# Attention stage: both exponentials ahead of the keeps, the output weights inside the turning product, sums one batch earlier, and 512 columns of x quantised by VectorE

## What is computed

```python
x = x + tanh(g_xattn[0]) * mlstm(layernorm(x), ctx, ctx, ifgate_w, ifgate_b, outnorm_w)
x = x + tanh(g_ffn[0])   * ffn_int8(layernorm(x), W1, b1, W2, b2)
x = x + tanh(g_xattn[1]) * align_by_time_warping(ctx, layernorm(x))
x = x + tanh(g_ffn[1])   * gated_experts(layernorm(x), ...)

def mlstm(q, k, v, ...):                      # 8 heads of 16 features
    log_d = lf[t] - lf[s] + i_pre[s]          # masked to s <= t
    m = max(log_d); d_mat = exp(log_d - m)
    s_mat = (q @ k.T) / 4 * d_mat
    denom = maximum(abs(sum(s_mat)), exp(-m)) + 5e-5
    h = (s_mat @ v) / denom
    rrms = rsqrt(mean(h * h) + 1e-6)          # per head
    return h * rrms * (1 + outnorm_w)

def qlinear(x, W, b):                         # twice in ffn_int8, gelu between
    scale = max((x.max() - x.min()) / 255, 1e-8)
    zp = clip(round(-x.min() / scale) - 128, -128, 127)
    xq = clip(round(x / scale) + zp, -128, 127)
    return ((xq - zp) @ wq.T) * (scale * sw) + b
```

## Time and profile before

| what | us |
|---|---|
| median of 3 runs (905.22 to 906.47) | 905.29 |
| the profiled execution, its own time | 905.67 |
| its span in the trace | 903.9 |

### The profile page before, as it was taken

One profiled execution on the slowest core, in us unless ns is written; L12 is line 12 of the kernel. 1 busy time (PEld: TensorE's weight loads), 2 busy tenths in 40 slices (PEclk: granted clock), 3 DMA queues, 4 the chain that ended last, 5 costly groups with the idle time before them and its releaser, 6 DMA issues.

```text
span 903.9 us, 16672 instructions
## 1 busy us (share of the span) xinstructions
PE 617.6 (68%) x5953; PEld 437.7 (48%) x6037; DVE 676.0 (75%) x1896; ACT 430.6 (48%) x892; POOL 196.3 (22%) x160
## 2 busy tenths in 40 slices
PE   4957999923425830000170479999999999999998
PEld 3943444411124630000160376777666777777776
DVE  6658467788979659899799875655666778878775
ACT  2425455457762363333560436556554445445543
POOL 3000168611436002221000036777000000000000
PEclk9999999975555985555585758999999999999999
DMA  7000000000001000000040000000000000001000
GB/s 195 24 1 0 2 1 1 2 1 1 1 14 33 1 1 1 9 12 12 14 140 0 1 1 1 2 2 1 1 2 13 2 13 0 12 0 35 0 13 13
DMA packets 20747, 13.12 MB, mean 15 GB/s; under 512 B 1580, under 2 KB 19240, under 8 KB 20680
## 3 DMA queue, kind: packets, MB, share of 16 engines
q1 hardware_dynamic: 20680, 12.27, 4.9%
HBM read 9.12 MB, written 2.10 MB: 12 GB/s over the span
## 4 chain that ended last, share of the span: by engine, by line
PE 55%; DVE 33%; issue 5%; ACT 5%; SPq 1%; DMA 1%; DVEq 0%; POOL 0%; ACTq 0%; POOLq 0%
PE PS L1494 7%; PE PS L1509 6%; PE PS L1511 6%; PE PS L1510 6%; PE PS L1495 6%; DVE Bm L1078 5%; DVE rowm L1090 5%; PE PS L1493 5%; DVE A L1073 4%; PE PS L1268 2%; PE PS L1334 2%; DVE hmm L1015 2%; DVE hmm L1016 2%; DVE A L728 2%; PE PS L1344 2%
## 5 line engine op out<-in xcount | busy, mean ns | idle before, releaser
L691 ACT ACTIVATE A<-PS,small_t 128x512 f32<-128x512 f32 x256 | 168.4, 688 | 123.9 <-PE PS L1495 122.4
L1509 PE MATMUL PS<-kT_w,A 128*128 128x128 bf16 x1024 | 174.8, 219 | 0.0
L1510 PE MATMUL PS<-kT_w,A 128*128 128x128 bf16 x1024 | 174.8, 219 | 0.0
L1511 PE MATMUL PS<-kT_w,A 128*128 128x128 bf16 x1024 | 174.7, 219 | 0.0
L1184 DVE TENSOR_TENSOR A<-A 128x512 bf16<-128x512 f32 x192 | 123.5, 690 | 12.0 <-ACT A L691 10.8
L1446 PE MATMUL PS<-identf,slab 128*128 128x128 f32 x128 | 21.1, 321 | 125.2 <-ACT xn_w L658 121.8
L1509 PEld LDWEIGHTS PS<-kT_w,A 128*128 128x128 bf16 x1024 | 100.2, 98 | 11.3 <-issue 4.6
L1510 PEld LDWEIGHTS PS<-kT_w,A 128*128 128x128 bf16 x1024 | 100.2, 98 | 6.6
L1494 PE MATMUL PS<-A,xn_w 128*128 128x512 bf16 (+1 forms) x256 | 98.2, 384 | 3.6 <-issue 0.4
L1511 PEld LDWEIGHTS PS<-kT_w,A 128*128 128x128 bf16 x1024 | 100.2, 98 | 0.0
L1495 PE MATMUL PS<-A,xn_w 128*128 128x512 bf16 (+1 forms) x256 | 98.3, 384 | 0.0
(11 more groups left out here) (287 smaller groups left out, 1279.1 us busy)
## 6 DMA issues: line engine op xcount, KB each, us to landing
slab<-in_L_ffn_w_dram SPq DMA_DIRECT2D x16, 256.0 KB, 3.1
xs<-in_x_dram SPq DMA_DIRECT2D x4, 512.0 KB, 6.3
cs<-in_ctx_dram SPq DMA_DIRECT2D x4, 512.0 KB, 6.8
out_dram<-xs SPq DMA_DIRECT2D x8, 256.0 KB, 2.3
A<-Bm SPq DMA_DIRECT2D x9, 64.0 KB, 2.0
xn_w<-in_L_ffn_W_dram SPq DMA_DIRECT2D x2, 256.0 KB, 2.9
A<-Bm SPq DMA_DIRECT2D x4, 36.0 KB, 1.8
A<-Bm SPq DMA_DIRECT2D x4, 24.0 KB, 1.8
```

Of the source, the lines that this page charges most:

```text
L691: act.activation(hf[:, e % 2, c, :], bank(c), ACT.Gelu_apprx_tanh, bias=b1).then_inc(S["h_gelu"], 1)
L1509: pe.matmul(o, hh[:, e % 2, c, t], w2h[:, e, c, :], start=(c == 0 and k == 0), stop=False, skip_group_check=True)
L1510: pe.matmul(o, hh[:, e % 2, c, t], w2l[:, e, c, :], start=False, stop=False, skip_group_check=True)
L1511: ins = pe.matmul(o, hl[:, e % 2, c, t], w2h[:, e, c, :], start=False, stop=(c == NC - 1), skip_group_check=True)
```

## The change

1. **ScalarE's order.** keep(b - 2) moves behind weights_exp(b, 1) and keep_turned(b - 1). squares(m) moves from b % 4 == 2 to 1.
2. **The turning product.** A matrix tmat of 128 x 132 for each half is built by GpSimd before the loop: 68 columns of the identity (four heads of 17) and 64 columns of the identity times onw_b. turn becomes two f32 products with it, keep copies 264 columns at a stretch, and each head's values are there plain and multiplied. normed reads the multiplied ones; the pass over onw_b goes, on GpSimd for six blocks and in late_norm for two. oall holds 16 sequences now, used in turn, for which keep waits at every fourth sequence from 16 on. TensorE waits for turn_made ahead of the loop.
3. **Sums one batch earlier** on VectorE: divisors at b % 4 == 1, mean_squares at 2; ln_stats(1, 0) at b = 24. Behind the loop the order is new as well, and TensorE issues turn(30) ahead of weigh(31).
4. **x's quantisation** is cut at 512, 1024, 2048 and 3072. The first 512 columns VectorE does alone in three passes, which raise xq_first; TensorE's first group waits for that. ab2_b's multiplication moves ahead of the loop.
5. **ScalarE** takes one Gelu of one column ahead of scale_x, roots(7) behind the first of its sixteen normalisations and the last square root behind the twelfth.

```diff
+XCUTS = [(512, 1024), (1024, 2048), (2048, 3072), (3072, 4096)]
...
+        oall = Bm[:, 4352:8576].rearrange("p (n w) -> p n w", n=16)
+        tmat = Bm[:, 10240:10504].rearrange("p (s c) -> p s c", s=2)
...
+            ident4 = identf[:].rearrange("p (j w) -> p j w", j=4)
+            for half in range(2):
+                pool.tensor_copy(tmat[:, half, 0:4 * VW].rearrange("p (j w) -> p j w", j=4), ident4[:, :, 0:VW])
             pool.wait_ge(S["gain_ready"], 1)
+            for half in range(2):
+                ins = pool.tensor_tensor(tmat[:, half, 4 * VW:4 * VW + 4 * DH].rearrange("p (j w) -> p j w", j=4), ident4[:, :, 0:DH],
+                                         onw_b[:, 64 * half:64 * half + 64].rearrange("p (j w) -> p j w", j=4), ALU.mult)
+            ins.then_inc(S["turn_made"], 1)
+            pool.wait_ge(S["turn_made"], 1)
...
             def onto(m):
-                t4 = four(osq[:, m % 2])
-                chain(pool.tensor_tensor(t4, t4, rep(onw_b[:], 4), ALU.mult), m, 4)
-                pool.tensor_tensor(g4(xs, m), g4(xs, m), t4, ALU.add).then_inc(S["x2_ready"], 1)
+                pool.tensor_tensor(g4(xs, m), g4(xs, m), four(osq[:, m % 2]), ALU.add).then_inc(S["x2_ready"], 1)
...
+                if b % 4 == 0 and b >= 16:
+                    act.wait_ge(S["x2_ready"], b // 4 - 3)
+                act.activation(oall[:, b % 16, :], bank(7, 0, 264), ACT.Copy).then_inc(S["o_kept"], 1)
...
                 weights_exp(b, 0)
-                if b >= 2:
-                    keep(b - 2)
                 weights_exp(b, 1)
                 if b >= 1:
                     keep_turned(b - 1)
-                if b % 4 == 2 and b >= 6:
+                if b >= 2:
+                    keep(b - 2)
+                if b % 4 == 1 and b >= 5:
                     squares(b // 4 - 1)
...
+            act.activation(gwarm, cst[:, 0:1], ACT.Gelu)
...
+            dve.tensor_tensor(ab2_b[:], ab2_b[:], tg[:, 2:3].to_broadcast([P, D]), ALU.mult)
             dve.wait_ge(S["expnm_ready"], 1)
...
                 if b % 4 == 0 and g >= 3:
-                    x_range(g - 3, 0)
+                    ins = x_range(g - 3, 0)
+                if b == 24:
+                    link(ins)
+                    ln_stats(1, 0)
+                if b % 4 == 1 and g >= 1:
+                    divisors(g - 1)
                 if b % 4 == 1 and g >= 3:
                     x_range(g - 3, 1)
                 if b % 4 == 2 and g >= 1:
-                    divisors(g - 1)
-                if b % 4 == 3 and g >= 1:
                     mean_squares(g - 1)
...
-                link(dve.tensor_tensor(th, heads(m)[:, :, 0:DH], last(f, DH), ALU.mult))
-                link(dve.tensor_tensor(four(t), four(t), rep(onw_b[:], 4), ALU.mult))
+                link(dve.tensor_tensor(by_head(t), gained(m), spread_out(f), ALU.mult))
...
+            first = xn_w1[:, 0:512]
+            dve.wait_ge(S["ln_half"], 1)
+            link(ts(first, first, qs[:, affine_x:affine_x + 1], MAGIC, ALU.mult, ALU.add))
+            link(ts(first, first, qs[:, affine_x + 2:affine_x + 3], qs[:, affine_x + 3:affine_x + 4], ALU.max, ALU.min))
+            ts(xq[:, 0:512], first, MAGIC, None, ALU.subtract).then_inc(S["xq_first"], 1)
...
+            pe.wait_ge(S["turn_made"], 1)
...
-                    ins = pe.transpose(bank(7, P * half, P * half + P), ot[:, b % 2, half, :], identf[:])
+                    ins = pe.matmul(bank(7, 132 * half, 132 * half + 132), ot[:, b % 2, half, :], tmat[:, half, :], start=True, stop=True)
...
+            turn(B - 2)
             weigh(B - 1)
-            turn(B - 2)
             turn(B - 1)
```

67 lines of the change are left out of this document (36 added, 31 removed).

## The result

| | median us | runs | profiled execution | span |
|---|---|---|---|---|
| before | 905.88 | 905.22 to 906.51, 4 | 905.67 | 903.9 |
| after | 900.25 | 898.39 to 900.47, 4 | 900.47 | 898.6 |

The ratio is 0.9933 with an interval of [0.9916, 0.9951]: faster by 0.67%, 5.6 us. The forecast was 8.8 us faster, 896.5, within 892.5 to 901.0. The direction and the range were right; 3.6 us of the forecast gain did not come (896.9 was worked out for the profiled execution, 900.47 was measured). The forecast by itself had 894 to 899, and 900.25 lies above that; it is inside the full range because that range also had room for the clock (rival D). It also happens to lie at the number of rival A (900.3), which the profile rules out.

The account below looks back on a forecast made before the run. The loop was taken as bound by a ring through ScalarE's keep, not quite by TensorE, and the tail largely by VectorE. Loop 3.8 gained, start 1.2 lost, tail 6.2 gained: 8.8 us, median 896.5, range 892.5 to 901.

Parts of the forecast that it names:

- rival D: Clock falls in TensorE's longer pause before the loop; one batch at 1.2 GHz costs 2.9 us: 899.4, chance 0.06.
- rival A: In the loop the wait only moves; something else holds the pitch at 3.26 us: 900.3, chance 0.10.
- The loop: Attention loop: ring through keep removed, turn 0.24 longer; pitch 3.26 to 3.13 us, 3.8 us gained over 29 batches.
- VectorE's hole: Loop: VectorE's moved work exceeds its 1.75 us of free time a batch by at most 0.5, inside 1.0 slack.
- The start: Before the loop TensorE waits for GpSimd to build tmat: 1.2 us lost, between 0.9 and 3.1.
- The tail: Behind the loop, from w' (start of weigh(30)): first hidden reduction at w' + 26.3 instead of w + 32.5, 6.2 us gained.
- Rival B: Tail: VectorE's queue sets the first hidden reduction; normalisations stretching throughout lose 2.5 us: 899.0, chance 0.13.
- Everything behind 216.36: From the first hidden-layer reduction (216.36 in the kernel before) on, same work in same order: no gain or loss.
- C: Loop: the turn costs no more than a transpose; pitch 2.89, 7.0 us more gained: 889.5, chance 0.05.
- G: rival A and Rival B together with a late loop start (3.1, 1.9 more): 904.7, chance 0.02.
- E: Loop: keep still holds back half 1's exponents, with a longer turn; pitch 3.62, 10.4 us lost: 910.7, chance 0.08.
- F: Loop: the turn's two products take the time of four, 0.89; pitch 3.56, 8.7 us lost: 909.0, chance 0.03.

Follow-up runs that it names:

- e3: Kernel before with only ScalarE's order changed (both exponentials and keep_turned ahead of keep): 894.77 us, ratio 0.9873.
- e4: Changed kernel with keep again between the two exponentials and squares, divisors and sums one batch later: 914.17 us (one run).
- e2: Changed kernel with the turning product undone (two transposes, keep of 136 columns, onw_b passes back, no tmat wait): 892.9 us, ratio 0.9838.
- e6: Changed kernel with VectorE's seven small statistics at b = 27 instead of b = 24: 899.88 us, ratio 0.9916.
- e5: Changed kernel with x quantised in four parts of 1024 columns, without the first 512 on VectorE alone: 901.99 us, ratio 0.9954.
- e9: Changed kernel without the single early Gelu, so its table loads when the first real one comes: 898.56 us (one run).
- e10: Changed kernel with seven warm products in TensorE's wait between transpose blocks 3 and 4 ahead of the expert stage: 899.42 us, ratio 0.9933.
- e1: Changed kernel with 28 instead of 16 idle warm products ahead of the attention loop: 898.39 us, ratio 0.9912.
- e11: Changed kernel with transposes, 28 warm products, most divisors and sums where they stood before, and seven warm products ahead of the expert stage: 887.89 us, ratio 0.98.

## Why the prediction was right, and where 3.6 us went

**The loop: right in mechanism, 0.02 short in size, one stall missed.** That keep between the exponentials was the wait is shown both ways: e3 takes it out alone and the pitch is 2.87, e4 puts it back (with squares, divisors and sums in their old batches) and the pitch is 3.64. The forecast was 3.13 a batch, by 2.89 and 0.24 for the turn. Measured: 2.87 (e3) and 0.28 (e2 against the changed kernel). The two errors nearly cancel: 29 x 0.02 = 0.5 us. The 0.24 came from products and transposes in a row of like shape, and took the two turns as the only difference; 0.04 more is what the real one costs in its place. The rule of the Trainium skill that spoke against the edit ("TensorE: Matmul & The Clock Gate", section Terms, transpose mode four times faster for FP32) is not borne out: from the turn to the next exponent are 0.55 instead of 0.28 us, a factor of two.

**The step that failed there** is the sentence on VectorE's hole: "the seven small statistics (the first takes 0.17, with their gaps some 1.0)". Their price was read at a place where GpSimd was idle, and they were moved beside GpSimd's passes. They took 2.85, and the stall of 0.59 is the pitch of 3.74. e6 shows it by moving them again, beside a GpSimd pass that does not stop them.

**The start: right for the wait, 1.32 for 1.2, wrong for the clock.** GpSimd's two products took 0.30 each, where 0.25 was forecast. What the step left out was its own rival D: the pause that it makes. TensorE's pause grew from 2.74 to 4.63, and at the restart the clock fell to 0.50. 1.3 of that growth is the wait; in this execution the warm products also ended 1.1 earlier, and onw_b was written 0.5 earlier. I had priced D at 2.9 (a whole batch at half speed) and given it 0.06, since the trace of before showed no fall at this place; but no row of it showed a longer pause here without one either, and the stretch behind the loop, with its longer pauses, showed 0.63. The chance was far too low. It cost 1.64 here (six exponents and the first scores), and 0.74 to 1.54 in e4, e5, e6, e9 and e10, which all have the wait. e1 removes it by shortening the pause alone. Without the wait the pause would have been some 3.3 (4.63 less 1.32, an estimate); e3, with 3.27, kept the clock, e2, with 3.87, lost it. So the wait makes the fall likely and is not its only cause.

**The tail: right.** mm's reduction at w' + 15.38 (15.55 to its end was forecast, it ended at 15.60), the first Gelu at w' + 23.05 (23.0), the first hidden reduction at w' + 26.36 (26.3); 6.1 us gained where 6.2 were forecast. That VectorE's queue and not ScalarE decides is shown from both sides: e5 turns it round, e9 takes 0.61 from ScalarE's side and moves the reduction by 0.12. Rival B, with its stretched normalisations, was not it: eight took 2.48 where 2.1 was forecast, the last four 1.90 as in the rows.

**Behind the tail: wrong.** "Everything behind 216.36 is the same work in the same order: nothing" holds for the work, not for the clock. The lead shrinks from 6.56 to 5.29. Of that 1.0 goes at the start of the expert stage, where the clock rises after nine products instead of six, and 0.3 between 507 and 517, which is not traced further. The table's last column speaks against a property of the change: over kernels with the same code there it runs from 336.9 to 339.1, one execution each, and among near copies of the changed kernel alone from 336.9 (e5, e9) to 338.5 (e6).

The sum of what was missed: 0.1 at the start, 1.6 by the clock, 0.5 by the pitch, 0.6 by the stall, 0.1 in the tail, 1.3 behind it, together 4.2; onw_b was written 0.54 us earlier in this execution (80.88, 81.42), which leaves 3.7. The distance between 896.9 and 900.47 is 3.6. The early onw_b is chance: without it the profiled execution would have stood at some 901.0, the very edge of the range.

**The other rivals.** A (pitch stays) and C (turn for nothing) fall by the pitch. G needs A and falls with it. E did not come about either, since the pitch is 3.15; e4 shows that its ring is real where keep stands between the exponentials: 3.64 a batch, 914.2 in all. F falls by the turn's 0.55.

**What stays open.** Why the clock rises when it does ahead of the expert stage, and why it fell back in e10 and e11, is not settled; the runs show when, not why. With it stays open why the expert stage took back 1.0 us. The differences between e1, e6, e10 and the changed kernel are shown by their traces, not by their times.
